# Two attention stages of a decoder: scores made first in even slots, read four units at a time into a ring of 12

## What is computed

```python
x = x + L0_attn(layernorm(x))            # 32 heads of 16, 8 kv heads, weights as signs with scales
x = x + L0_xattn(layernorm(x), ctx)      # 32 heads of 128 on the 64 context rows
x = x + L0_ffn(layernorm(x))             # per block of 32, only the best hidden unit counts
x = x + L1_attn(layernorm(x))            # 32 heads of 16, one kv head, causal with ALiBi
x = x + L1_xattn(layernorm(x), ctx)      # 32 heads of 16, 8 kv heads, mask over keys
x = x + L1_ffn(layernorm(x))             # dense product plus 2 of 8 low-rank experts
```

```python
scores = q @ k.T / sqrt(16)              # 64 x 64
scores = scores + alibi or mask          # not in L0_attn
p = softmax(scores)
out = p @ v                              # then a product with the output weights
```

## Time and profile before

| | us |
|---|---|
| median of 3 runs | 2214.14 (2213.44 to 2216.16) |
| the profiled execution | 2213.81 |
| its span | 2212.0 |
| TensorE matmuls busy | 2118.3 (96%) |
| DVE busy | 1344.8 (61%) |
| ACT busy | 1028.0 (46%) |
| POOL busy | 902.6 (41%) |

### The profile page before, as it was taken

The page is one execution under the profiler, slowest core; times in us unless marked ns, Lnnn a source line. Parts: engine busy times, 40 slices in busy tenths (PEclk is TensorE's granted clock), DMA queues, the critical chain, the costliest instruction groups (busy, mean ns, idle before and its releaser), DMA issues. The chain is left out here.

```text
span 2212.0 us, 45005 instructions
## 1 busy us (share of the span) xinstructions
PE 2118.3 (96%) x18686; PEld 1718.5 (78%) x18686; DVE 1344.8 (61%) x2350; ACT 1028.0 (46%) x1754; POOL 902.6 (41%) x675
## 2 busy tenths in 40 slices
PE   6997999999999999999999999999998899999998
PEld 5665888888887888888888877888887677777766
DVE  6985544443334453444433558797785788888856
ACT  5774553545535455354543552111102667667632
POOL 2787241432414414143241345122122668778611
PEclk9998999999999999999999999999999899999999
DMA  4000111110112101111010123000002100100002
GB/s 168 2 21 21 48 33 55 39 47 32 40 39 77 58 21 39 39 39 58 21 40 36 44 66 98 1 0 0 0 1 76 31 7 21 50 27 11 2 1 77
DMA packets 23374, 82.06 MB, mean 37 GB/s; under 512 B 4112, under 2 KB 6288, under 8 KB 17040
## 3 DMA queue, kind: packets, MB, share of 16 engines
q1 hardware_dynamic: 23184, 79.33, 10.6%
HBM read 74.08 MB, written 4.19 MB: 35 GB/s over the span
## 5 line engine op out<-in xcount | busy, mean ns | idle before, releaser
L2644 PE MATMUL xat_TP<-shared_rounded 128*128 128x512 f32 x1024 | 321.6, 395 | 0.1
L2316 POOL TENSOR_TENSOR xat_T<-xat_T,xat_mask 128x512 f32<-128x512 f32 x64 | 82.1, 1295 | 479.3 <-DVE xat_T L2406 479.3
L104 PE MATMUL xat_G<-xat_xnT_hi,shared_rounded 128*128 128x512 f32 x768 | 244.5, 391 | 0.0
L2303 POOL TENSOR_TENSOR shared_rounded<-shared_landing,shared_rounded 128x2048 fp32r<-128x2048 f32 x39 | 179.5, 4609 | 152.4 <-ACT shared_rounded L2160 152.4
L2644 PEld LDWEIGHTS xat_TP<-shared_rounded 128*128 128x128 f32 x1024 | 188.3, 188 | 44.6 <-issue 6.2
L2644 PE MATMUL xat_TP<-shared_rounded,xat_oT_lo 128*128 128x512 f32 x512 | 199.6, 390 | 0.0
L2397 DVE RECIPROCAL xat_q_inv_rms<-xat_OT 128x16 f32<-128x16 f32 x32 | 8.3, 258 | 304.7 <-PE xat_OT L2569 304.7
L104 PE MATMUL ffn_H<-shared_rounded 128*128 128x448 f32 (+1 forms) x816 | 178.8, 368 | 3.7 <-DVE ffn_h_kept L1469 2.5
L1401 POOL TENSOR_TENSOR ffn_one_hot<-ffn_one_hot,ffn_block_rank 128x448 f32<-128x448 f32 x64 | 75.3, 1176 | 253.6 <-DVE ffn_one_hot L1450 253.6
L1377 ACT ACTIVATE shared_rounded<-ffn_TP 128x384 fp32r<-128x384 f32 x64 | 34.8, 544 | 293.4 <-PE ffn_Y L1526 246.7
L104 PEld LDWEIGHTS ffn_H<-shared_rounded 128*128 128x128 f32 x816 | 152.3, 188 | 20.8 <-DVE ffn_h_kept L1469 5.0
(11 more groups left out here) (363 smaller groups left out, 4959.5 us busy)
## 6 DMA issues: line engine op xcount, KB each, us to landing
shared_landing<-in_Cq_q SPq DMA_DIRECT2D x16, 1024.0 KB, 4.8
shared_landing<-in_Cq_o SPq DMA_DIRECT2D x16, 1024.0 KB, 4.8
shared_landing<-in_Cq_kv SPq DMA_DIRECT2D x8, 1024.0 KB, 8.2
shared_landing<-in_ctxT_paired SPq DMA_DIRECT2D x4, 1024.0 KB, 7.1
two_ctxT_raw<-in_ctxT SPq DMA_DIRECT2D x8, 512.0 KB, 4.0
shared_landing<-in_w1T SPq DMA_DIRECT2D x8, 448.0 KB, 3.7
shared_landing<-in_w SPq DMA_DIRECT2D x7, 512.0 KB, 3.7
out<-X SPq DMA_DIRECT2D x6, 512.0 KB, 3.0
```

The costliest lines, as they stand in the source:

```text
L104: last = eng.matmul(out, a, b, start=(n == 0), stop=(n == len(steps) - 1))
L2303: return eng.tensor_tensor(w[1][:, :, :], landed[:, :, :], w[0][:, :, :].bitcast(F32), ALU.subtract)
L2316: eng.tensor_tensor(T[:, n, :, :], T[:, n, :, :], mask[:, :].unsqueeze(1).to_broadcast([P, ROWS, SEQ]), ALU.add)\
L2644: last = eng.matmul(TP[m % 2][:, :], x, w, start=(n == 0), stop=(n == len(steps) - 1))
```

## The change

In `small_attention` the ring gets 12 units. DVE reads four units (pairs s and s + 1) in even slots from slot 2 on, and none in odd ones; the maxima of two stay two units a slot. TensorE makes the scores ahead of the first turn in even slots.

```diff
@@ -265,7 +265,7 @@
-    RING = 8
+    RING = 12
@@ -942,15 +942,14 @@
                 if s < LASTP:
-                    if sign:
-                        max_pair(s)
-                    else:
-                        take_scores(2 * s)
-                        take_scores(2 * s + 1)
-                if s < LASTP:
-                    if sign:
-                        shift_pair(s)
-                    else:
+                    for p in (s,) if s < 2 else (s, s + 1) if s % 2 == 0 else ():
+                        if sign:
+                            max_pair(p)
+                            shift_pair(p)
+                        else:
+                            take_scores(2 * p)
+                            take_scores(2 * p + 1)
+                    if not sign:
                         find_max(2 * s)
                         find_max(2 * s + 1)
@@ -1143,10 +1142,10 @@
             for s in range(SLOTS):
+                if s < LASTP and s % 2 == 0:
+                    scores(s)
                 if LAG <= s < LASTP + LAG:
                     turn(2 * (s - LAG))
-                if s < LASTP and s % 2 == 0:
-                    scores(s)
                 if LAG + 2 <= s < LASTP + LAG + 2 and s % 2 == 1:
                     values((s - LAG - 2) // 2)
```

## The result

The changed kernel takes 2236.38 us (median of 4 runs, 2234.18 to 2243.49) against 2213.79 (4 runs): a ratio of 1.0107, 95% interval 1.0089 to 1.0125. I had said 2226, between 2212 and 2235. The direction was right and the cost almost twice what I summed.

The account below looks back on a forecast made before the run. The prediction took TensorE to set the pace, with DVE close behind. Terms of +9.4 us in two and +2.4 in gqa, added to 2213.8, gave 2225.6, stated as 2226; the 8-in-10 range was 2212 to 2235.

Parts of the forecast that it names:

- L892's term: gqa's first group: x3 already waits 1.84 us for DVE's L892, now behind a further pair of reads; +2.4 us.
- gqa, last group and end: gqa's last group: scores ahead of A fill its wait and the clock stays higher; about -3.8 us, bounds 0 and -6.
- reading ahead lets DVE [...] follow, -0.6: gqa's last group: DVE, busy 34.9 of 52 us, can follow thanks to early reads; -0.6 us.
- rival 4: DVE's burst becomes the bound: four reads delay sums, turns may wait for POOL; +1 per group, 2236 us, chance 0.05.
- Covered are slot 6 of each group: In two, slot 6's second turn (B) has work between it and the first (A), so no 0.90 us charge.
- the turn after B is late too: In two, the turn after a slot's second turn adds about 0.2 us at 9 places; +1.8 us.
- -6.5 for x3's wait: In two, early reads end x3's seven waits for DVE's addition of y1 to X, 6.7 us; taken as -6.5.
- 18 us for the 20 waits: In two, 20 uncovered second turns (B) each wait for ACT's copy of the first (A), 0.90 us; +18.0 us.
- the ring at nothing: Ring of 12: 8 KB more per partition, no instruction; costed at 0, between 0 and +0.2 us.
- rival 3: Two, slot 4, first three groups: paired waits lower TensorE's clock; three or four places, some 2.5 us each, 2234, chance 0.10.
- the bounds of B alone: Second turns (B) at 27 places cost 0.78 to 1.1 us each instead of 0.90; -3 to +5 us.
- the case as summed: Whole kernel: the summed terms hold, +11.8 us, 2226 us, bounds 2220 to 2233, chance 0.58.

Follow-up runs that it names:

- experiment 1: Kernel before with only TensorE's new order (scores ahead of the first turn in even slots), old reads and ring of 8: 2232.5 us, ratio 1.0080.
- experiment 8: Kernel before with the new order in gqa's last group alone, reads and ring as before: 2211.8 us, ratio 0.9994.
- experiment 10: Changed kernel without the early reads in gqa's last group: 2231.58 us, ratio 1.0084 to the kernel before.
- experiment 5: Changed kernel with DVE's inverse sums in gqa made between the two pairs' reads in even slots: 2240.14 us, ratio 1.0115 to the kernel before.
- experiment 6: Changed kernel with TensorE's old order in slot 6 of each of two's eight groups: 2234.83 us, ratio 1.0093 to the kernel before.
- experiment 2: Changed kernel with TensorE's old order back, so early reads and ring of 12 alone: 2223.95 us, ratio 1.0045 to the kernel before.
- experiment 7: Changed kernel with two's new order only in even slots that have an item between the turns: 2228.09 us, ratio 1.0067 to the kernel before.
- experiment 11: Kernel before with eight buffers of turned probabilities instead of four and the new order in gqa's last group: 2205.78 us, ratio 0.9973.

## Why the prediction was right or wrong

Stretch by stretch, from the table (scores' 0.53 put back):

| | forecast | measured | |
|---|---|---|---|
| ahead of gqa's first scores | 0 | +1.3 | clock, ahead of the change |
| gqa, first group | +3.0 | +4.8 | L892's term right; clock 0.90, against 0.96 before |
| gqa, groups 2 and 3 | +3.2 | +4.1 | |
| gqa, last group and end | -3.8 | +1.0 | wrong sign; -1.8 without the early reads |
| xat and ffn | 0 | -1.3 | spread |
| two | +9.4 | +13.0 | slot 6 costed at 0 |
| sum | +11.8 | +22.9 | |

**The failed step is the last group of gqa**, "reading ahead lets DVE [...] follow, -0.6. Together about -3.8". For the order alone the forecast held up to slot 30: experiments 1, 8 and 10 each show -4.1 there. Behind slot 30 the term had nothing, and in experiments 1 and 10 2.3 are lost again (1.2 of it idle time), so that group and end are -1.8 together (-2.4 in experiment 5, -3.4 in 8, where the clock was higher). The early reads take that away and more (+1.0), and I had given them the sign of a gain, -0.6. Of the 4.8 us by which this term is wrong, 2.8 are the early reads, measured against experiments 1 and 10, and 2.0 is the end of the stage. How, in the changed kernel (DVE and POOL from slot 24 on, then TensorE's turn A of slot 28):

```profile
167.56 1.29 DVE L847 TENSOR_REDUCE gqa_row_max<-gqa_S 128x8 f32<-128x512 f32 x2 [1.63 <-PE gqa_S L1096]
...
171.16 1.28 DVE L854 TENSOR_TENSOR gqa_T<-gqa_S,gqa_row_max 128x512 f32<-128x512 f32 x2
172.35 1.21 DVE L860 TENSOR_REDUCE gqa_row_sum<-gqa_T 128x16 f32<-128x1024 f32 x1
...
173.93 2.04 POOL L745 TENSOR_TENSOR gqa_T<-gqa_T,gqa_row_inv 128x512 f32<-128x512 f32 x2 [4.68 <-DVE gqa_row_inv L865]
...
186.69 0.66 PE L1107 MATMUL gqa_TP<-ident,gqa_T 128*128 128x128 f32 x4 [1.54 <-POOL gqa_T L745]
```

and POOL's product of the same slot in experiment 5:

```profile
175.95 2.04 POOL L745 TENSOR_TENSOR gqa_T<-gqa_T,gqa_row_inv 128x512 f32<-128x512 f32 x2 [2.84 <-DVE gqa_row_inv L865]
```

DVE idles 1.63 us for scores, then reads for 4.8 us, and only then makes the sums. POOL stands 4.68 us for them (2.84 in experiment 5). It has two products and a low part to make per slot, and in most slots the scaling and adding of y; it is busy 3.9 to 4.0 of every 4 us from 176 to 192, and turns wait for it. Behind the longest of these waits (1.54) the clock falls as well: 0.57 between 188 and 192, and 0.94 from slot 24 to 30 in all four kernels with the new order and early reads there, against 1.00 without the reads. That the reads ahead of the inverse are the step is tested by experiment 5: with the inverse ahead of the second reads the stretch has its -4.1 again, and waits for POOL from slot 24 to 30 are 1.1 us in place of 2.8. I had seen this mechanism as rival 4, gave it 0.05 and placed it in two, where DVE has room; it came in gqa's last group, where POOL, busy 41.3 of 52 us in the earlier trace rows, has least. I read that row for DVE's 34.9 alone. Rival 4's time of 2236 is the measured one by luck: it was added from +1 in every group, and the runs have the loss elsewhere, and slot 6 beside it.

**The second is slot 6 of two.** "Covered are slot 6 of each group" was said of B, and B is covered. The term "the turn after B is late too" I applied only where transposes or nothing follow B. It is the same chain with ACT's longer slot, and it cost 4.7 us (experiment 6). Without it two's +13.0 would be +8.3, and I had +9.4. That these lie close is partly luck. The sum had -6.5 for x3's wait, which the early reads do end, but by themselves they gave nothing in two (+2.6, experiment 2); and it charged 18 us for the 20 waits, which are worth 6 once the reads are early (experiment 7).

**Right:** B at 1.43 us behind A and 0.90 us of cost, the turns' waits in two (23.6, I said some 25), the end of the wait for L901, the ring at nothing, TensorE's start in gqa (+2.4 for L892: 1.84 became 4.24). I had the wait of turns in gqa at 25 too, and it is 19.6, plus 4.2 for POOL.

**The clock, rival 3.** In the changed kernel's profile the clock is 1.00 in both stretches of two above, so the rival is no part of this result. But in the profile of the kernel with gqa's early reads in the last group alone the clock fell at a place that I named, slot 4 of the third group: behind waits of 0.78 and 0.90 the clock is 0.62 between 1850 and 1854, and the scores' distance there is 2.2 us more than in the kernel before, where the changed kernel's is 0.6 more:

```profile
1847.89 0.63 PE L1107 MATMUL two_TP<-ident,two_T 128*128 128x128 f32 x4 [0.78 <-ACT two_PT L619]
1849.41 0.86 PE L1107 MATMUL two_TP<-ident,two_T 128*128 128x128 f32 x4 [0.90 <-ACT two_PT L619]
```

Seven profiled kernels have that pair of waits, in three groups each; in one passage of the 21 the clock fell. So the Trainium skill ("TensorE: Matmul & The Clock Gate", "A second HAM failure mode: psum-queue depth-cycling") names something that can happen here. As a rule for such waits it did not hold, and by this count 0.10 for three places at once was too much rather than too little.

**The range** missed by 1.4 us. It was built from the bounds of B alone; gqa's last group had 0 and -6 as its bounds, both gains, though the reads there had no row. A bound on the side of a loss, one read pair (2.4 us) at three places, would have carried it past the result. The 2233 for the case as summed was also added up short: 2225.6 with the 5 of the B's and the 3.8 of the last group is 2234.

## What to carry to other kernels

When work is moved earlier on an engine with a fixed list, write down everything that now stands behind it and, for each, the engine that waits for it and how busy that one is; a gain for one reader was a loss for the next in experiments 2 and 5. A wait that is added or removed is worth its length only up to the waits behind it (20 waits of 0.90 us were worth 6 us in experiment 7), so follow the chain to the next turn of the same buffer, not only to the instruction that waits. Look for a wait that leads back to the engine it started from, here A's copy for TensorE's values and TensorE's next turn for A's copy: a second set of buffers took 0.25% off, which no reordering did. And split a stretch that got shorter or longer into busy and idle time, with its granted clock, before calling it a wait: two thirds of the -4.1 were clock.

## What the runs showed of the hardware

In some places the clock fell behind a pause of TensorE in one execution and not in another. Ahead of gqa's first scores, where the change has touched nothing yet, the changed kernel had this q0 product and first scores:

```profile
24.21 3.43 PE L104 MATMUL gqa_G<-shared_rounded 128*128 128x512 f32 x8
28.42 0.70 PE L1096 MATMUL gqa_S<-gqa_Kbd,gqa_qT 32*64 32x128 f32 x32 [0.78 <-ACT gqa_qT L588]
```

and experiment 6, with the same instructions up to there, this:

```profile
24.27 2.09 PE L104 MATMUL gqa_G<-shared_rounded 128*128 128x512 f32 x8
27.14 0.70 PE L1096 MATMUL gqa_S<-gqa_Kbd,gqa_qT 32*64 32x128 f32 x32 [0.78 <-ACT gqa_qT L588]
```

though TensorE had been idle longer in the second (1.35 us ahead of 22.9, against 0.64). So the scores came 1.3 us later. The same at two's end: a wait of 2.65 us, behind one of 2.8 or 2.9, passed at full clock in the changed kernel and was followed by the low level in experiment 6:

```profile
2133.00:2137.00 4.00, 3.73 (x9) 2.96 (x10) 2.19 (x4) 0.00 (x0) 1.70 (x3) 0.50 0.02 4
2137.00:2141.00 4.00, 4.00 (x16) 3.21 (x15) 2.16 (x8) 0.60 (x1) 0.35 (x1) 0.71 0.00 0
```

There it made a product of 3.02 us one of 5.49. What decides between the two isn't settled by these runs.

In another place the runs agree. From slot 24 to 30 of gqa the clock is 0.88 in the three kernels with the old code there (before, the ring alone, the change in two alone), where turns wait 0.87 and then 1.47 or 1.48 us, and 1.00 in the five with the new order and no early reads there (experiments 1, 5, 8, 10 and 11).

The reader's rule for one profiled execution: a difference of a stage below some 2 us is not evidence unless the granted clock of both stretches has been compared. A stretch that repeats to 0.1 us from kernel to kernel, as the -4.1, is evidence, even where a part of it is clock.
